# Self attention in rounds of four heads: scores from 32-row slices, probabilities transposed by DMAs

## The reference

```python
q = jnp.einsum('btc,hcd->bhtd', x, Wq) + bq        # 16 heads of 32
k = jnp.einsum('btc,hcd->bhtd', x, Wk) + bk
v = jnp.einsum('btc,hcd->bhtd', x, Wv) + bv
scores = jnp.einsum('bhtd,bhsd->bhts', q, k) * scale
probs = jax.nn.softmax(scores + causal, axis=-1)
y = jnp.einsum('bhts,bhsd->bhtd', probs, v)
...
x = x + _L0_attn_ref(_layernorm(x), ...)           # self attention
x = x + _L0_xattn_ref(_layernorm(x), ctx_1024, ...)
x = x + _L0_ffn_ref(_layernorm(x), ...)
```

## Time and profile before

| | us |
|---|---|
| median of 3 runs (lowest to highest) | 1655.2 (1653.52 to 1657.58) |
| the profiled execution, its own time | 1660.59 |
| its span | 1658.8 |
| first stage, up to | 160.8 |
| self attention, from there up to | about 976 |
| third stage, from there up to | 1658.8 |

### The profile page before, as it was taken

How to read it: one execution, slowest core, us unless ns; L and a number is a source line. 1 busy time by engine, 2 the same in 40 slices (tenths; PEclk the granted TensorE clock), 3 DMA queues, 4 the chain that set the end, 5 groups by cost and what they waited for, 6 DMA issues and landing times. The chain is left out here.

```text
span 1658.8 us, 29018 instructions
## 1 busy us (share of the span) xinstructions
PE 1547.3 (93%) x10720; PEld 1289.4 (78%) x10720; DVE 1221.4 (74%) x2417; ACT 831.7 (50%) x1992; POOL 407.7 (25%) x357
## 2 busy tenths in 40 slices
PE   7886898999999999999999847999999999999998
PEld 5665777888788888888888635878887887888886
DVE  4345486888888788888877757787878787878765
ACT  4443476677677776767777623232322222323211
POOL 2231112112021211202121134342424243333310
PEclk9998899999999999999999977999999999999999
DMA  9998442342444434244333424122222222222000
GB/s 320 317 320 248 106 106 62 77 129 64 105 121 88 109 77 130 62 119 112 90 78 77 140 104 159 70 77 77 77 78 82 77 77 78 77 77 83 26 14 26
DMA packets 75195, 178.95 MB, mean 108 GB/s; under 512 B 9392, under 2 KB 9520, under 8 KB 71344
## 3 DMA queue, kind: packets, MB, share of 16 engines
q1 hardware_dynamic: 75056, 177.07, 36.9%
HBM read 76.37 MB, written 50.33 MB: 76 GB/s over the span
## 5 line engine op out<-in xcount | busy, mean ns | idle before, releaser
L643 ACT ACTIVATE a_probs<-a_score,a_neg_max 128x384 f32<-128x384 f32 (+3 forms) x512 | 264.5, 527 | 137.4 <-DVE a_neg_max L732 136.7
L732 DVE TENSOR_REDUCE a_neg_max<-a_score 128x1 f32<-128x384 f32 (+3 forms) x352 | 208.8, 635 | 74.8 <-PE a_score L849 74.5
L652 ACT ACTIVATE a_pt_hi<-a_turned 128x512 f16<-128x512 f32 (+1 forms) x352 | 181.3, 561 | 67.7 <-PE a_turned L859 66.5
L739 DVE TENSOR_TENSOR a_pt_lo<-a_turned,a_pt_hi 128x512 f16<-128x512 f32 (+1 forms) x352 | 207.7, 631 | 0.0
L859 PE MATMUL a_turned<-ident,a_probs 128*128 128x128 f32 x1280 | 185.9, 282 | 22.8 <-DVE a_pt_lo L739 11.5
L597 POOL TENSOR_TENSOR a_y<-a_y_sum,a_y_rec 128x128 f32<-128x128 f32 x128 | 51.3, 401 | 587.7 <-DVE a_y_sum L750 585.7
L859 PEld LDWEIGHTS a_turned<-ident,a_probs 128*128 128x128 f32 x1280 | 138.0, 142 | 37.4 <-ACT a_probs L643 30.4
L1204 ACT ACTIVATE b_probs<-b_probs 128x1024 f32<-128x1024 f32 x32 | 33.9, 1060 | 197.0 <-DVE b_probs L1323 197.0
L841 PE MATMUL a_score<-a_stack 96*128 96x384 f32 (+3 forms) x512 | 126.5, 354 | 2.8 <-DMA a_stack<-a_qk 2.8
L878 PEld LDWEIGHTS a_out_y<-a_v,a_pt_hi 128*128 128x128 f16 x1280 | 97.8, 99 | 30.2 <-DVE a_pt_lo L739 14.5
L878 PE MATMUL a_out_y<-a_v,a_pt_hi 128*128 128x96 bf16 x1280 | 118.9, 210 | 1.4 <-DVE a_pt_lo L739 0.9
(11 more groups left out here) (189 smaller groups left out, 4068.2 us busy)
## 6 DMA issues: line engine op xcount, KB each, us to landing
a_stack<-a_qk SPq DMA_DIRECT2D x384, 128.0 KB, 2.4
m_dram<-c_m_out SPq DMA_DIRECT2D x8, 2048.0 KB, 13.5
vw_dram<-shared SPq DMA_DIRECT2D x32, 512.0 KB, 8.3
shared<-m_dram SPq DMA_DIRECT2D x8, 2048.0 KB, 8.6
b_vw_raw<-vw_dram SPq DMA_DIRECT2D x8, 2048.0 KB, 8.3
c_w_raw<-w_group_dram SPq DMA_DIRECT2D x7, 1280.0 KB, 11.0
xn<-x_dram SPq DMA_DIRECT2D x8, 1024.0 KB, 5.5
a_x_res<-x_dram SPq DMA_DIRECT2D x8, 1024.0 KB, 5.2
```

The lines of the kernel that those rows point to most:

```text
L643: ins = nc.scalar.activation(probs[:, s % 2, k * width:(k + 1) * width], score[s % 2][:, k * width:(k + 1) * width], ACT.Exp, bias=neg_max ...
L652: nc.scalar.activation(pt_hi[:, s % 4, 0:width], turned[s % 2][:, 0:width], ACT.Copy).then_inc(pt_hi_ready, 1)
L732: nc.vector.tensor_reduce(neg_max[:, c:c + k], score[s % 2][:, 0:k * width].rearrange("p (h s) -> p h s", h=k), AX, ALU.max, negate=True). ...
L739: nc.vector.tensor_tensor(pt_lo[:, s % 4, 0:width], turned[s % 2][:, 0:width], pt_hi[:, s % 4, 0:width], ALU.subtract).then_inc(pt_ready, 1)
```

## The change

- A batch is 12 rounds: per quad one for row tiles 0 and 1 together, one for tile 2, one for tile 3 (`ROUND_TILES`). A round has all four heads, as two units of two heads each.
- `stack` and its DMAs are gone. Scores read queries and keys where they lie, 32 rows a head, with three matmuls per tile and head in place of one; each head writes its own bank of the 4-bank tensor `score`. There is one such tensor: the scores of a round wait for the exponentials of the round before.
- No transposes of probabilities on PE, and no bank `turned`. The high part of the untransposed probabilities is written by ACT for even units (`parts_hi`) and by DVE for odd ones, the low part by POOL for all (`parts_lo`), and SP transposes both by one DMA a unit (`turn_parts`). `weigh` comes two rounds behind (`BEHIND`).
- `beside_rounds` spreads the dense steps over the rounds by their length alone. `AHEAD`, what is computed before the first scores, has two uses less. The adding of the output bias on POOL is cut into four. The parts lie in the memory into which the third stage's first operand is loaded, so this load now waits for the last transposes.

```diff
+ROUND_TILES = ((0, 1), (2,), (3,))
+def beside_rounds(uses, rounds, length):
+    out, done = [[] for _ in range(rounds)], 0
+    for b, kind, n in uses:
+        for k in range(STEPS[kind]):
+            out[min(rounds - 1, int(done / length * rounds))].append(((b, kind, n), k))
+            done += LENGTH[kind]
     return out
...
+    PROB_SLOTS, PART_SLOTS, TURN_SLOTS = 4, 4, 6
+    BEHIND = 2
+    AHEAD = [(0, "xt", k) for k in range(KT)] + [(0, *u) for u in (("qk", 0), ("qk", 1), ("v", 0))]
     def early(b):
+        uses = [(b, "v", 1)] + [(b - 1, "yt", 1)] * (b > 0) + [(b, "qk", 2)] + [(b - 1, "yt", 2)] * (b > 0)
+        uses += [(b, "qk", 3), (b, "v", 2)] + [(b - 1, "yt", 3)] * (b > 0)
+        return uses + [(b, "v", 3), (b, "qk", 4), (b, "qk", 5)] + [(b - 1, "o", 0)] * (b > 0)
     def late(b):
+        uses = [(b, "qk", 6), (b, "qk", 7)] + [(b + 1, "xt", 0)] * (b + 1 < B)
         for t in range(1, TT):
             uses += [(b - 1, "o", t)] * (b > 0) + [(b + 1, "xt", t)] * (b + 1 < B)
+        return uses + [(b + 1, "qk", 0), (b + 1, "qk", 1), (b + 1, "v", 0)] * (b + 1 < B) + [(b, "yt", 0)]
...
+            def turn_parts(u):
+                sp.wait_ge(parts_ready, u + 1)
+                if u >= TURN_SLOTS:
+                    sp.wait_ge(weighed, u - TURN_SLOTS + 1)
+                cols = 4 * columns_of(u // 2)
+                sp.dma_start_transpose(turned[:, u % TURN_SLOTS, 0:cols // P, :],
+                                       parts[:, u % PART_SLOTS, 0:cols]).then_inc(turned_landed[u % TURN_SLOTS], 16)
...
             sp.wait_ge(vw_stored, XG * 64 + 64)
+            for u in range(2 * B * NR - PART_SLOTS, 2 * B * NR):
+                sp.wait_ge(turned_landed[u % TURN_SLOTS], landed(u))
             sp.dma_start(m_raw, m_dram[0].rearrange("p g m -> p (g m)")).then_inc(m_loaded, 16)
...
+            def parts_lo(u):
+                pool.wait_ge((hi_by_act, hi_by_dve)[u % 2], u // 2 + 1)
+                nc.gpsimd.tensor_tensor(part(u, 1), probs[:, u % PROB_SLOTS, 0:2 * columns_of(u // 2)], part(u, 0),
+                                        ALU.subtract).then_inc(parts_ready, 1)
...
+            for r in range(B * NR):                      # ACT
+                for u in units_of(r):
+                    exps(u)
+                parts_hi(2 * r)
+                for use in FILLED[r - 1] if r else []:
                     if use[1] == "v":
                         values_second(use)
+                for use in FILLED[r]:
                     high_part(use)
...
+            for r in range(B * NR):                      # DVE
+                b, at = divmod(r, NR)
+                if r:
+                    parts_hi(2 * r - 1)
+                for u in units_of(r):
+                    row_max(u)
+                if is_round(r - BEHIND - 1):
+                    outputs(r - BEHIND - 1)
+                for use in FILLED[r]:
                     low_part(use)
...
+            def scores(r):                               # PE
+                b, q = r // NR, quad_of(r)
+                if r % len(ROUND_TILES) == 0:
+                    pe.wait_ge(gemm_drained, drained((b, "qk", 2 * q + 1)))
+                if r:
+                    pe.wait_ge(probs_ready, 2 * r)
+                for n, (of_q, of_k) in enumerate([(Q_HI, K_HI), (Q_HI, K_LO), (Q_LO, K_HI)]):
+                    at = 0
+                    for i in tiles_of(r):
+                        width = (i + 1) * P
+                        for j in range(HQ):
+                            rows = slice(j * HD, (j + 1) * HD)
+                            nc.tensor.matmul(score[:, j, at:at + width], qk[q % 2][rows, of_q, i * P:(i + 1) * P],
+                                             qk[q % 2][rows, of_k, 0:width], start=n == 0 and at == 0, stop=False)
+                        at += width
...
+            for r in range(B * NR):
+                scores(r)
+                mask(r)
+                for step in BESIDE[r]:
                     step_of_product(*step)
+                for u in units_of(r - BEHIND):
+                    weigh(u)
```

More of the change, by code:

```diff
@@ L466, in self_attention @@
         Q_LO, Q_HI, K_HI, K_LO = range(4)
-        stack = [sb(f"stack{n}", [3 * HD, 2, HQ, T], F32R) for n in range(2)]
         v_rest = sb("v_rest", [P, 2, D], F32)
@@ L478, in self_attention @@
         gemm = [pb(f"gemm{n}") for n in range(2)]
-        score = [pb(f"score{n}") for n in range(2)]
-        turned = [pb(f"turned{n}") for n in range(2)]
+        score = ctx.enter_context(nc.psum_tensor("a_score", [P, HQ, 512], F32))
         out_y = [pb(f"out_y{n}") for n in range(2)]
@@ L826, in whole_product @@
                     step_of_product(use, k)
-            def scores(s):
-                b, n = divmod(s, NU)
-                q, i, heads = UNITS[n]
-                if n % PQ == 0:
-                    pe.wait_ge(stacked[q % 2], (b * 2 + q // 2 + 1) * STACK_DMAS)
-                if s > 1:
-                    pe.wait_ge(probs_ready, s - 1)
-                width = (i + 1) * P
-                st = stack[q % 2]
-                for k, j in enumerate(heads):
-                    at = k * width
-                    nc.tensor.matmul(score[s % 2][:, at:at + width], st[:, 0, j, i * P:(i + 1) * P], st[:, 1, j, 0:width],
-                                     start=k == 0, stop=False)
@@ L844, in mask @@
-            def mask(s):
-                q, i, heads = UNITS[s % NU]
-                width = (i + 1) * P
-                for k in range(len(heads)):
-                    at = k * width
-                    last = nc.tensor.matmul(score[s % 2][:, at + i * P:at + width], ident_bf[:, :], causal_bf[:, :],
-                                            start=False, stop=k == len(heads) - 1)
-                last.then_inc(score_full, 1)
-            def turn(s):
-                q, i, heads = UNITS[s % NU]
-                pe.wait_ge(probs_ready, s + 1)
-                if s > 1:
-                    pe.wait_ge(pt_ready, s - 1)
-                for c in range((i + 1) * len(heads)):
-                    last = nc.tensor.transpose(turned[s % 2][:, c * P:(c + 1) * P], probs[:, s % 2, c * P:(c + 1) * P],
-                                               ident[:, :])
-                last.then_inc(turned_full, 1)
@@ new lines, in mask, with weigh @@
+            def mask(r):
+                for j in range(HQ):
+                    at = 0
+                    for i in tiles_of(r):
+                        last = nc.tensor.matmul(score[:, j, at + i * P:at + (i + 1) * P], ident_bf[:, :], causal_bf[:, :],
+                                                start=False, stop=i == tiles_of(r)[-1])
+                        at += (i + 1) * P
+                    if j % 2:
+                        last.then_inc(score_full, 1)
+            def weigh(u):
+                r, half = divmod(u, 2)
+                b, q = r // NR, quad_of(r)
+                pe.wait_ge(turned_landed[u % TURN_SLOTS], landed(u))
+                if half == 0:
+                    g = b * GROUPS + group_of(r, tiles_of(r)[-1])
+                    if g > 1:
+                        pe.wait_ge(y_summed, g - 1)
+                    if q % 2 == 0:
+                        pe.wait_ge(v_ready, b * 4 + q + tiles_of(r)[-1] // 2 + 1)
+                blocks = columns_of(r) // P
+                for k in range(2):
+                    j, first = 2 * half + k, 0
+                    at = j * V3
+                    for i in tiles_of(r):
+                        g = group_of(r, i)
+                        for t in range(i + 1):
+                            hi, lo = (turned[:, u % TURN_SLOTS, (2 * n + k) * blocks + first + t, :] for n in range(2))
+                            val = v[:, t, q * HQ + j, :, :].rearrange("p k d -> p (k d)")
+                            nc.tensor.matmul(out_y[g % 2][:, at:at + V3], hi, val, start=t == 0, stop=False)
+                            last = nc.tensor.matmul(out_y[g % 2][:, at:at + 2 * HD], lo, val[:, 0:2 * HD],
+                                                    start=False, stop=t == i)
+                        first += i + 1
+                last.then_inc(weighed, 1)
```

372 lines of the change are left out of this document (155 added, 217 removed).

## The result

The changed kernel takes 1760.1 us (median of 4 runs, 1756.9 to 1763.6) against 1655.7 for the kernel before on the same chip: 1.063 times, 95% interval 1.061 to 1.066. It is slower, inside the range, 50 us above the forecast. The profiled execution took 1763.6 us.

What follows compares the result with a forecast made beforehand. PE bounds the kernel before at 96.0 us a batch; after, bank waits make it 98.8. That gives 1637 us, plus 78 for scores, switches, DVE's copy and clock: 1715 profiled, 1710 median, range 1630 to 1800.

Steps and rivals of the forecast that it cites:

- The wait that decides: Dense steps: PE waits for banks until DVE's low parts of uses filled in the same round, 18 to 22 us a batch.
- the clock: PE after its waits: falls to half clock put 4 us a batch on the path, +32 us (0 to +80).
- DVE's order: DVE's copy before the maxima delays them after late low parts, rounds 9 and 0: 0.9 a batch, +7 us.
- scores and switches: PE's scores: imperfect overlap of fours, +3.0 a batch, +24 us; changing between 32 and 128 rows, +15 us (0 to +31).
- Rounds without the clock: Twelve rounds of batches 1 to 6, priced by work, chains and bank waits: 98.8 us a batch together.
- The first batch: Batch 0, with no `o` or `yt` of a batch before and fewer collisions: 78 us.
- Start and end: First scores at about 176.3 us; last exponentials to the next stage 20 us, against 20.5 before.
- 1: Scores on PE: row slices overlap wholly, switching is free, the clock holds; 1632 us, faster; chance 0.20.
- 2: Scores on PE: weight loads of the slices queue at 0.11 us, +12.1 a batch; 1783 us, slower; chance 0.20.
- 3: Scores on PE: nothing overlaps, +27 us a batch, +216; about 1900 us; chance 0.07.
- 4: Probabilities: transposing DMAs can't keep up; at 80 GB/s a batch takes 131 us, kernel about 1890; chance 0.06.
- rival 5: Dense steps: bank waits don't bite because ACT drains earlier; some 82 us a batch, about 1505 us; chance 0.05.

Runs made afterwards that it cites:

- experiment 1: Changed kernel with a fixed table of two whole uses per round in place of `beside_rounds`: 1640.7 us, 0.990 of the kernel before.
- experiment 3: Changed kernel with 44 to 90 extra small matmuls, results overwritten, ahead of the use before each same-round bank wait: 1707.4 us.
- experiment 2: Changed kernel with DVE normalising the next batch's x ahead of the low parts in rounds 5 and 6: 1749.5 us.
- experiment 11: Also e11_late_load: e7_plan_order with the last batch's 1 MB x_res load behind the last transposes and its additions behind the last low parts: 1545.1 us.
- e7_plan_order: Changed kernel with two whole uses per round, ACT's high parts before its copy, DVE's copy and low parts last, x_res added one round later: 1554.9 us.
- experiment 5: Changed kernel with the score loops turned round, head outermost, so matmuls on the same 32 rows stand together: 1796.8 us (one run).

## Why the prediction was right, and where it was off

- **The wait that decides.** Right: PE stands for the banks, on the low parts named, 26 us a batch where I expected 18 to 22; the uses that wait are those listed. Taking the waits inside a round away brings 119 us (experiment 1).
- **The sum of a batch.** I had 98.8 + 3.0 scores + 1.9 switches + 0.9 DVE + 4.0 clock = 108.6 us. Measured 112.7 in batch 3. With the clock held, experiment 3 has 104.5, which leaves 8.2 for the clock (7.4 on the mean of batches 1 to 6): twice my term, and the error that is left in the sum. The granted clock was 0.89 and not the 0.85 that I expected, so it was no deeper fall. I counted 0.7 us on the path of the 1.7 that each fall costs; six waits and 7.4 to 8.2 us make 1.2 to 1.4 a wait. PE ran at half clock for nearly all products behind each wait (571.40 to 575 in round 7), and most of that was on the path. That all else came to 104.6 by my sum and to 104.5 measured is luck, since two errors cancel in it: DVE's order, 3.6 too low, and scores and switches, 2.9 too high.
- **Rounds without the clock.** Against 9.75, 9.75, 7.7, 9.9, 6.3, 7.7, 6.3, 10.6, 8.9, 6.6, 6.3, 9.0 stand 11.0, 9.8, 7.6, 10.6, 6.5, 7.6, 6.6, 13.2, 9.1, 7.0, 6.5, 9.1. Nine agree within 0.4. Round 7 is 2.6 over: its maxima stand behind two normalisings (1.20) and a copy (0.55) that wait behind a late low part. Rounds 0 and 3 are 1.2 and 0.7 over; in the trace of experiment 3 their maxima too stand behind low parts and a copy, in round 0 the long one of 1.74 us. This is the term "DVE's order", 0.9 a batch by me and some 4.5 by these traces, of which experiment 2 tested the normalising alone (2.4 us a batch with what followed from it). I had looked for it in rounds 9 and 0 and not in 7.
- **Scores in fours.** Over-priced. To the first mask they take 0.89, 0.73 and 0.91 us for rounds A, B and C at full clock (the last from 521.58 to 522.49), 10.1 a batch, and those times contain the change back to 128 rows. (14 of the 32 rounds A begin at half clock and take 1.58; that is in the term of the clock.) From last weighing matmul to first score pass 0.12 us, at a usual distance of 0.04 to 0.07. So scores and both changes take about 11 us, 2 over my low end of 9.0, where I had put 4.9. By the Trainium skill (TensorE: Matmul & The Clock Gate, Part 3), whose 3.07 I had turned into an estimate of 12 us for scores alone, they would be slower than they are; for these shapes the measurement decides. By the Trainium skill (TensorEngine Tiling (Array Packing), Key Properties) a change of the tiling mode drains TensorE. The trace doesn't contradict it: from the last score of 384 columns, 0.22 us by the price before, to the first mask 0.26 us pass. Whether those 0.04 us are a drain no run shows; the cost is small.
- **The first batch.** 98.9 us, where I had 78 + 9.75. I had priced it in one line, by the same reckoning and without its list of rounds. It has waits of 5.2 and 4.8 us for `qk` in rounds 7 and 9 and one of 5.6 us for DVE's sum of the results, queued behind low parts.
- **Start and end.** First scores at 175.7, predicted 176.3; that this agrees so well is in part luck, since versions with the same code up to there have them at 170.2 to 176.1. The end was predicted about as long as before and is 13.5 us longer. I had the last transposes at 4 us and did not ask what SP issues just ahead of them; experiment 11 shows 7 us of it. That the 2 MB load would be no trouble was right, the 1 MB load was not looked at.
- **The total.** Rounds 33 us over (first batch 11, the others 22) and the end 14, which makes up the 48 us between 1715 and the profiled 1763.6. The forecast's sign and mechanism hold. The terms that were mis-sized are the clock (4.0 for 7.4 to 8.2 a batch), DVE's order (0.9 for some 4.5), scores and switches (4.9 for 2), the first batch (88 for 99) and the end (20 for 34). Slower by 104 us was measured where 55 was forecast, so about half of the size was foreseen, and it would be less had scores and switches not been 23 us too high.
- **Rivals.** 1 was right about the slices and the switches, wrong on the clock, and so not the outcome. 2, 3 and 4 are out. 5 is out for the changed kernel, since the waits bite. Its picture of a batch holds once plan and orders take the waits away: batches 1 to 6 of e7_plan_order take 83.6 us on the mean, where it had 82. That version came to 1555 and not to rival 5's 1505 for two other reasons: the stretch of scores is 661 us, where 1505 leaves some 630 for it, above all in the first and last batch, and the end is 15 us longer.

The end in e11_late_load is still 8 us longer than in the kernel before. The load of x for the next stage waits for the last stores of this one; it is issued 28.9 us after the last exponentials there, and 20.4 before. GpSimd's last low parts end 5.8 us and the last transpose lands 10.5 us after the last exponentials, two steps that the kernel before does not have in this form. The 2 MB load lands at 851.0, 9 us ahead of the load of x, and is not on this path.

Not settled: how much of the end is its low clock, what GpSimd's work costs by way of DVE's copies, and why two-tile rounds lose much of the overlap of slices in experiment 5 while the others keep it.

## What to carry to other kernels

When a change halves the shared buffers between a producer and its drain (here one `score` tensor for four heads, and a use drained inside the round that needs its bank), count the loop of one round through every engine, including what stands ahead of each drain in that engine's own program, and put drains ahead of work that nobody waits for. Price each wait of TensorE of several microseconds with the work behind it at half clock and on the path (here 1.2 to 1.4 us a wait, where I took 0.7). And look at what the DMA queue has just been given ahead of a transfer on the path: a prefetch of 1 MB, issued early, cost 7 us here.

## What the runs showed of the hardware

- Four 32-row slices of 4-byte matmuls into four banks run in about the time of one: twelve of 384 columns in 0.73 us to the next kind of matmul, 24 of 128 and 256 columns in 0.89, at full clock.
- The order of issue matters less than expected: three matmuls in a row on the same rows, then the next slice, still overlapped (0.77 us for twelve), six in a row only in part (1.90 us for 24, where none would give 3.0).
- Work that only keeps TensorE busy pays here: 350 idle matmuls a batch took the granted clock of batch 3 from 0.89 to 1.00 and 48 us off the stage.
- A transposing DMA of 384 to 512 KB in half precision lands after 4.2 us, a plain one of the same bytes after 2.6 to 2.9; in steady batches of 82 to 113 us the difference doesn't show in the time, at the end of the stage it is about 3 us.
- Two transposes issued 0.5 and 3.6 us behind a load of 1 MB landed after 7.5 us (median) and made TensorE wait 5.5; without the load ahead they landed after 3.9.
- DVE's copy of 768 or 1024 columns to half precision takes 0.54 to 0.70 us while GpSimd is idle; of those that started while GpSimd worked, 22 of 46 took 0.9 to 2.0.
